# First stage of a decoder layer: context loaded and squared batch by batch, distances sent to DRAM and back per batch

## The reference

```
# 1 linear causal attention with one head of 16, tiled 16 times before the projection
q, k, v = split(x @ qkv_w.T + qkv_b);  wei = where(tril, q @ k.T, 0)
x = layernorm(x + tile(wei @ v, 16) @ proj_w.T + proj_b)
# 2 per batch: Euclidean distances D[77, 256] of context rows to x rows, dynamic time warping over D,
#   backtracking, and the context rows added to the x rows that the path gives them
D = sqrt(max(|c|^2 + |x|^2 - 2 c.x, 0));  R = dtw(D);  path = backtrack(R)
x = layernorm(context_rows_added_along(path) + x)
# 3 product-key memory: batch norm, query, two top-8 of 64, top-8 of 64 pairs, gathered down/up rows
x = layernorm(x + memory(x))
```

## Time and profile before

| | |
|---|---|
| median of 3 runs | 2913.73 us (2905.39 to 2916.35) |
| the profiled execution, its own time | 2907.08 us |
| its span, first to last instruction | 2905.3 us |
| first block | 0 to 201 us of the span |
| first warping row | 207.4 us |
| mean granted TensorE clock | 0.956 of full speed |

### The profile page before, as it was taken

One profiled execution on the slowest core, in us unless ns is written; L12 is line 12 of the kernel. 1 busy time (PEld: TensorE's weight loads), 2 busy tenths in 40 slices (PEclk: granted clock), 3 DMA queues, 4 the chain that ended last, 5 costly groups with the idle time before them and its releaser, 6 DMA issues.

```text
span 2905.3 us, 104629 instructions
## 1 busy us (share of the span) xinstructions
PE 2652.9 (91%) x43108; PEld 2293.1 (79%) x43108; DVE 2210.9 (76%) x7510; ACT 761.9 (26%) x1340; POOL 857.1 (30%) x670
## 2 busy tenths in 40 slices
PE   6961167799999999999999999999999999999996
PEld 5851145688888888888888888888888888888895
DVE  5668966877777777777777777777777778777744
ACT  4740055322222222222222222222222222222210
POOL 1330142233333333333333333333333333333332
PEclk9985589999999999999999999999999999999997
DMA  5550337400000000000000000000000000000000
GB/s 174 172 161 23 65 112 177 72 13 13 11 13 10 13 12 12 13 13 13 14 13 13 13 14 13 13 14 13 13 14 13 13 13 14 13 14 13 10 10 12
DMA packets 84630, 99.34 MB, mean 34 GB/s; under 512 B 6189, under 2 KB 74702, under 8 KB 84046
## 3 DMA queue, kind: packets, MB, share of 16 engines
q1 hardware_dynamic: 84190, 92.94, 11.5%
HBM read 65.13 MB, written 27.79 MB: 32 GB/s over the span
## 4 chain that ended last, share of the span: by engine, by line
PE 82%; issue 7%; DVE 1%; DMA 1%; ACT 1%; POOL 0%; POOLq 0%; DVEq 0%; SPq 0%; ACTq 0%
PE bank L1078 32%; PE bank L1112 31%; PE bank L1096 9%; PE bank L1049 8%; PE bank L767 1%; DMA x_again<-x_scratch 1%; PE bank L770 1%; PE bank L1064 1%; PE bank L1036 1%; DVE hot L1295 0%; ACT x_sb L727 0%; POOL best L664 0%; DMA x_scratch<-x_sb 0%; DVE shared L1307 0%; ACT L1197 0%
## 5 line engine op out<-in xcount | busy, mean ns | idle before, releaser
L1015 POOL TENSOR_TENSOR hot<-hot,valsT 128x512 f32<-128x512 f32 x512 | 733.0, 1451 | 1662.8 <-DVE hot L1295 1662.8
L1078 PE MATMUL bank<-x2T,shared 128*64 128x128 f32 x16384 | 951.4, 274 | 4.6 <-issue 3.1
L1078 PEld LDWEIGHTS bank<-x2T,shared 128*64 128x64 f32 x16384 | 889.8, 137 | 26.6 <-issue 11.9
L1295 DVE TENSOR_TENSOR hot<-places,valsT 128x1024 f32<-128x1024 f32 x512 | 647.6, 1305 | 0.2 <-issue 0.2
L1112 PE MATMUL bank<-up,shared 64*128 64x256 f32 x4096 | 449.4, 379 | 1.5 <-DVE shared L1307 1.5
L1112 PE MATMUL bank<-up,gelh 64*128 64x256 f32 x4096 | 446.4, 377 | 0.0
L1112 PEld LDWEIGHTS bank<-up,shared 64*128 64x128 f32 x4096 | 397.1, 188 | 58.9 <-issue 11.4
L1112 PEld LDWEIGHTS bank<-up,gelh 64*128 64x128 f32 x4096 | 395.2, 187 | 56.2 <-issue 11.5
L1096 PE MATMUL bank<-hot 64*64 64x64 f32 x16384 | 303.1, 224 | 30.9 <-POOL hot L1015 16.3
L1096 PEld LDWEIGHTS bank<-hot 64*64 64x64 f32 x16384 | 267.9, 137 | 79.7 <-issue 79.7
L1307 DVE TENSOR_TENSOR shared<-bank,shared 128x512 f32<-128x512 f32 x256 | 164.7, 685 | 176.8 <-PE bank L1096 176.4
(11 more groups left out here) (151 smaller groups left out, 2169.5 us busy)
## 6 DMA issues: line engine op xcount, KB each, us to landing
x_scratch<-x_sb SPq DMA_DIRECT2D x64, 256.0 KB, 2.1
xT_sb<-in_xT SPq DMA_DIRECT2D x32, 256.0 KB, 2.9
x_sb<-in_x SPq DMA_DIRECT2D x32, 256.0 KB, 3.0
x_again<-x_scratch SPq DMA_DIRECT2D x32, 256.0 KB, 2.8
x_tile<-x_scratch SPq DMA_DIRECT2D x32, 256.0 KB, 3.9
up<-in_table SPq DMA_DIRECT2D x2, 4096.0 KB, 37.0
yo<-x_scratch SPq DMA_DIRECT2D x32, 256.0 KB, 3.0
out_y<-yo SPq DMA_DIRECT2D x32, 256.0 KB, 2.0
```

Source lines behind the costliest of these rows:

```text
L1015: pool.tensor_tensor(lo, lo, valsT[:, par, 2, TQ * q:TQ * (q + 1), None].to_broadcast([P, TQ, NK]), ALU.mult).then_inc(gated_ready, 1)
L1078: mm = pe.matmul(ps_h[q % 2][half(c), i, :], dnT[:, k, lo // 2, half(lo % 2)], x2T[:, par, k, c, :], start=(k == 0), stop=(k == CC - 1))
L1295: dve.tensor_tensor(hot[:, q % SLOTS], places[:, None, None, :].to_broadcast([P, 2, TQ, NK]), valsT[:, par, 0:2, TQ * q:TQ * (q + 1), None ...
```

## The change

It touches the first block and the hand-over to the second.

- Context: instead of four parts, each batch's rows (77 runs of 1 KB) and columns (256 runs of 308 B, into a buffer with two slots) are loaded by two DMAs, `load_ctx`, lag 4 in SyncE's order, last in its step. `norms` squares one batch a step at lag 3; `ctx_scale` at lag 3.
- Distances: after `store_dist` (lag 7) of a batch, `load_cost` (lag 8) waits for that store and loads the batch's distances into their place, `cost[b:P:NB, :]`: four partitions, four runs of 20 KB. The four loads at the start of the second block go; its VectorE waits for no load.
- Lags: TensorE's highest lag is 4 instead of 7, ScalarE's 4 instead of 9, VectorE's 4 instead of 8; orders of the stages in the lists are new; the head's lag is 1 instead of 2. ScalarE's qkv is cut in two (`qk`, `v`) with `std` between. VectorE has four drains in a step instead of two.
- SyncE's code is written out for all steps, with no loop.
- Start: the first xT load comes ahead of the weights; TensorE waits for two early memsets (`pads`) instead of all constants; ScalarE asks for Sqrt once before its data is there; the proj reduction is done in two halves, in VectorE's steps 0 and 1, and attn of batch 0 waits for both.
- `table_init` is raised twice: once after `acc`'s first memsets, which is all the first warping row needs, and once after the rest.

```diff
...
@@ -232,7 +236,7 @@
                 return st.enter_context(nc.sbuf_tensor(name, shape, dt))
             projT = sa("projT", [HS, C * NHEAD])
-            ctx_cols = sa("ctx_cols", [P, CC, NB, S2])
+            ctx_cols = sa("ctx_cols", [P, CC, 2, S2])
             ctxm2 = sa("ctxm2", [P, 2, CC, RP])
             x_sb = sa("x_sb", [P, 2, NT, C])
             xT_sb = sa("xT_sb", [P, 2, CC, T])
@@ -252,7 +256,7 @@
             x1sq = sa("x1sq", [P, CC, T])
             x1sum = sa("x1sum", [P, 2, T])
             dist_sb = sa("dist_sb", [RP, 2, T])
-            sq_scr = sa("sq_scr", [S2, 8, C])
+            sq_scr = sa("sq_scr", [S2, C])
             ps_qkv, ps_v = bank[0][0:2 * GAP + HS, 0:T], bank[6][:, 0:NT * P].rearrange("p (t d) -> p t d", t=NT)
             ps_wei = bank[1][:, 0:3 * P].rearrange("p (k t) -> p k t", k=3)
@@ -272,18 +276,6 @@
                     return ap[bass.ds(b, 1)].rearrange("a p t c -> (a p) t c")
                 def load_xT(b, par):
-                    if isinstance(b, int) and b == 1:
-                        sp.wait_ge(consts, 1)
-                        for dst, src in ((projT[:, :], projT_d), (proj[HS:HS + 1, :], projb_d),
-                                         (gamma[:, :], gamma_d), (beta[:, :], beta_d)):
-                            sp.dma_start(dst, src).then_inc(p_in, 16)
-                    if isinstance(b, int) and 2 <= b < 2 + NB // 8:
-                        some = slice(8 * (b - 2), 8 * (b - 1))
-                        sp.dma_start(ctx_rows[:, some, :], ctx_rows_d[some].rearrange("b s c -> s b c"))\
-                            .then_inc(ctx_in[b - 2], 16)
-                        sp.dma_start(ctx_cols[:, :, some, :],
-                                     ctx_cols_d[:, some].rearrange("(k p) b s -> p k b s", k=CC))\
-                            .then_inc(ctx_in[b - 2], 16)
                     if later(b, 2):
                         sp.wait_ge(qkv_mm, b - 1)
                     sp.dma_start(xT_sb[:, par], one(xTb, b)).then_inc(xT_in[par], 16)
@@ -297,36 +289,59 @@
                     sp.wait_ge(x1_ready, b + 1)
                     sp.dma_start(one(x1b, b), x1_sb[:, par]).then_inc(x1_out[par], 16)
+                def load_ctx(b, par):
+                    if later(b, 2):
+                        sp.wait_ge(norm_seen, b - 1)
+                        sp.wait_ge(ctxm2_ready, b - 1)
+                    sp.dma_start(ctx_rows[:, b, :], ctx_rows_d[b]).then_inc(rows_in[par], 16)
+                    sp.dma_start(ctx_cols[:, :, par, :], ctx_cols_d[:, b].rearrange("(k p) s -> p k s", k=CC))\
+                        .then_inc(cols_in[par], 16)
+
                 def store_dist(b, par):
                     sp.wait_ge(root_ready, b + 1)
-                    sp.dma_start(dist_d[bass.ds(b, 1)].rearrange("a (i j) -> (a i) j", i=RP),
-                                 dist_sb[:, par]).then_inc(dist_out[par], 16)
-
+                    sp.dma_start(dist_d[b].rearrange("(i j) -> i j", i=RP), dist_sb[:, par, :]).then_inc(dist_out[par], 16)
+
+                def load_cost(b, par):
+                    sp.wait_ge(dist_out[par], dmas(b, par))
+                    sp.dma_start(cost[b:P:NB, :], dist_d[b].rearrange("(g f) -> g f", g=NG)).then_inc(cost_in[par], 16)
+
+                load_xT(0, 0)
                 for part in range(3):
                     of = slice(HS * part, HS * (part + 1))
                     at = slice(GAP * part, GAP * part + HS)
                     sp.dma_start(wqkv[:, :, at], wqkvT_d[:, of].rearrange("(k p) d -> p k d", k=CC)).then_inc(w_in, 16)
                     sp.dma_start(bias[at, :], bqkv_d[of]).then_inc(w_in, 16)
-
-                pipeline(sp, [(load_xT, 0), (load_x, 5), (store_x1, 7), (store_dist, 10)], 12)
+                load_xT(1, 1)
+                sp.wait_ge(pads, 1)
+                for dst, src in ((projT[:, :], projT_d), (proj[HS:HS + 1, :], projb_d),
+                                 (gamma[:, :], gamma_d), (beta[:, :], beta_d)):
+                    sp.dma_start(dst, src).then_inc(p_in, 16)
+
+                for i in range(1, NB + 9):
+                    for stage, lag, first in ((load_xT, 0, 2), (load_x, 1, 0), (store_x1, 5, 0), (store_dist, 7, 0),
+                                              (load_cost, 8, 0), (load_ctx, 4, 0)):
+                        if first <= i - lag < NB:
+                            stage(i - lag, (i - lag) % 2)
                 for par in range(2):
                     sp.wait_ge(x1_out[par], 16 * NB // 2)
-                    sp.wait_ge(dist_out[par], 16 * NB // 2)
+                    sp.wait_ge(cost_in[par], 16 * NB // 2)
             @block.gpsimd
             def _(pool):
                 pool.memset(wqkv[:, :, HS:GAP], 0.0)
                 pool.memset(wqkv[:, :, GAP + HS:2 * GAP], 0.0)
+                pool.memset(proj[:, :], 0.0)
+                pool.memset(eps_col[:, :], EPS)
+                pool.drain()
+                pool.nop().then_inc(pads, 1)
                 pool.memset(ones[:, :], 1.0)
                 pool.memset(qT[:, :, :], 0.0)
                 pool.memset(kT[:, :, :], 0.0)
                 pool.memset(vT[:, :, :], 0.0)
                 pool.memset(v_sb[:, :, :, :], 0.0)
-                pool.memset(proj[:, :], 0.0)
                 pool.memset(headT[:, :, :], 1.0)
                 pool.memset(ctxm2[:, :, :, :], 0.0)
                 pool.memset(ctx_norm[:, :], 0.0)
-                pool.memset(eps_col[:, :], EPS)
                 pool.memset(ident[:, :], 0.0)
                 pool.memset(causal[:, :, :], 1.0)
                 pool.iota(iota_i[:, :], [[1, T]], base=0, channel_multiplier=0)
@@ -361,6 +376,8 @@
                 def turn_v(b, par):
                     pe.wait_ge(vT_ready, b + 1)
+                    if not later(b, 1):
+                        pe.wait_ge(consts, 1)
                     if later(b, 1):
                         pe.wait_ge(v_ready, b)
                     for t in range(NT):
@@ -390,7 +407,7 @@
                 def attn(b, par):
                     pe.wait_ge(head_ready, b + 1)
                     if not later(b, 1):
-                        pe.wait_ge(setup_v, 1)
+                        pe.wait_ge(setup_v, 2)
                     if later(b, 1):
                         pe.wait_ge(sum_done, b)
                     for t in range(NT):
@@ -419,19 +436,21 @@
                     pe.wait_ge(sq_ready, b + 1)
                     pe.matmul(ps_dist, ones[:, :], x1sum[:, par, :], start=False, stop=True).then_inc(dist_mm, 1)
-                pe.wait_ge(consts, 1)
+                pe.wait_ge(pads, 1)
                 pe.wait_ge(w_in, 16 * 6)
-                pipeline(pe, [(head, 2), (qkv, 0), (wei, 1), (turn_v, 1), (attn, 3), (turn_x1, 6), (dist, 7)], 10)
+                pipeline(pe, [(qkv, 0), (head, 1), (dist, 4), (wei, 0), (turn_v, 0), (attn, 1), (turn_x1, 2)], 6)
             @block.scalar
             def _(act):
-                def qkv(b, par):
+                def qk(b, par):
                     act.wait_ge(qkv_mm, b + 1)
                     if later(b, 2):
                         act.wait_ge(wei_mm, b - 1)
                     act.activation(qT[0:HS, par, :], ps_qkv[0:HS, :], ACT.Identity, bias=bias[0:HS, :])
                     act.activation(kT[0:HS, par, :], ps_qkv[GAP:GAP + HS, :], ACT.Identity, bias=bias[GAP:GAP + HS, :])\
                         .then_inc(qk_ready, 1)
+
+                def v(b, par):
                     if later(b, 2):
                         act.wait_ge(v_mm, b - 1)
                     act.activation(vT[0:HS, par, :], ps_qkv[2 * GAP:, :], ACT.Identity, bias=bias[2 * GAP:, :])\
@@ -453,14 +472,12 @@
                 def ctx_scale(b, par):
-                    if not later(b, 1):
-                        for part in ctx_in:
-                            act.wait_ge(part, 32)
+                    act.wait_ge(cols_in[par], dmas(b, par))
                     if later(b, 2):
                         act.wait_ge(dist_mm, b - 1)
                     rest(act, act_rests)
                     act.activation(ctxm2[:, par, :, 0:S2],
-                                   ctx_cols[:, :, bass.ds(b, 1), :].rearrange("p k a s -> p k (a s)"),
+                                   ctx_cols[:, :, par, :],
                                    ACT.Copy, scale=-2.0).then_inc(ctxm2_ready, 1)
                 def head(b, par):
@@ -478,9 +495,11 @@
                     act.wait_ge(dist_ready, b + 1)
                     act.activation(dist_sb[:, par, :], dist_sb[:, par, :], ACT.Sqrt).then_inc(root_ready, 1)
+                act.wait_ge(pads, 1)
+                act.activation(sd1[:, 0, 0:1], eps_col[:, :], ACT.Sqrt)
                 act.wait_ge(consts, 1)
                 act.wait_ge(w_in, 16 * 6)
-                pipeline(act, [(root, 9), (head, 2), (qkv, 0), (wei_off, 1), (ctx_scale, 6), (x1_cols, 6), (std, 4)], 12)
+                pipeline(act, [(qk, 0), (std, 2), (v, 0), (head, 1), (wei_off, 0), (ctx_scale, 3), (root, 4), (x1_cols, 2)], 6)
```

(40 more changed lines are left out.)

## The result

The changed kernel takes 2925.86 us in the median (2923.79 to 2927.7, 5 runs) against 2913.15 before: ratio 1.0062, 95% interval 1.0049 to 1.0074. The changed kernel is slower, by some 0.6%, where 2908 us with a range of 2889 to 2920 was forecast. In the profiled executions the span goes from 2905.3 to 2922.8 us, 17.5 more.

A forecast was written before the change was run, and what follows sets the result against it. TensorE bounds the first block at 4.99 us a step; late column loads were to make it 5.57. Earlier hand-over -20.3 plus 14.5 lost gave -5.8 us: 2901.3 profiled, 2908 us by the median, range 2889 to 2920.

The forecast's parts named there:

- What a late column load costs: First block, batches 4 to 28: late context columns delay the residual two steps on; step 5.57 us, 14.5 us lost.
- Rival 4: SyncE's new queue: something else, such as SyncE waiting at the distance load for a store; called cheap; chance 0.05.
- Filling: Start of the first block: first matmul at 5.8 us, first full step (step 4) at 27.9 us.
- Full steps: First block's steps from batch 4: 4.99 us each by the compute engines, 5.57 where the column load is late.
- Emptying and hand-over: End of first block: at 4.99 us a step, VectorE starts the first warping row at 187.1, 20.3 us earlier.
- By the compute engines alone the step stays at 4.99 us; shorter lags cost nothing there: First block's full step: TensorE's work sums to 4.99 us, VectorE's to 4.0, GpSimd's to 1.77.
- The price of 1.53 us: Per-batch distance load: a 20 KB row takes 1.53 us on its DMA engine, ahead of the context columns.
- The gain of 20.3 us: First warping row at 187.1 instead of 207.38 if the first block's step stays at 4.99 us.
- rival 1: The distance load hides: step stays at 4.99 us, 20.3 us gained, 2893 us by the median; chance 0.25.
- rival 2: Context columns' 308-byte runs are dear, 0.1 us each: step 6.25 us, 2925 us by the median; chance 0.12.

The follow-up runs named there:

- e2: Changed kernel without the per-batch distance load, four loads at the start of the second block instead: 2928.48 us, ratio 1.0072 to the kernel before.
- e1: Changed kernel with the distance store one step earlier in SyncE's order (lag 6 instead of 7): 2921.38 us, ratio 1.0046 to the kernel before.
- e9: Changed kernel with four slots and four semaphores instead of two for the distances, SyncE's order untouched: 2923.60 us, ratio 1.0062 to the kernel before.
- e5: Changed kernel with x1 store and distance store ahead of the x load in SyncE's step, lags kept: 2895.53 us, ratio 0.9962 to the kernel before.
- e11: e7 with the scale ahead of `dist` in VectorE's list: 2889.26 us, ratio 0.9945 to the kernel before.
- e7: Changed kernel with both stores ahead of the x load and the context load at lag 3: 2894.74 us, ratio 0.9957 to the kernel before.
- e8: e7 with each batch's distances loaded a second time into unused memory, as four rows of 20 KB: 2917.80 us, ratio 1.0038 to the kernel before.
- e10: e7 with each batch's distances loaded a second time into unused memory, as 80 rows of 1 KB: 2895.16 us, ratio 0.9961 to the kernel before.
- e3: Changed kernel with the distance store at lag 6 and distances loaded at the start of the second block: 2904.40 us, ratio 0.9984 to the kernel before.
- e6: e5 without the per-batch distance load, four loads at the start of the second block instead: 2895.57 us, ratio 0.9962 to the kernel before.

## Why the prediction was wrong

**Which step failed.** The sum that gives the step, under "What a late column load costs": "2p = 5.68 + 5.45 = 11.13 and p = 5.57 us". It is the right working of a ring that comes second. The one on top, VectorE's `dist` waiting for the distance store of b - 2, has a turn of one step, 6.35 us, and was not laid out. In the forecast stores were bytes on the DMA engines and a latency; who waits for their landing was asked for the column load alone. e2 and e1 show it from both sides: the step stays without the distance load, and the wait goes with the store a step earlier; e9 takes the buffer wait away and the step falls to 5.93; e5 shows that the place of the stores behind the waiting x load is the cause.

**Rival 4 was nearest and was priced away.** It put a wait for a store at SyncE and called it cheap, as "stores land in 1.7 us and are issued a step before". Both halves failed. The slot is wanted, for a step of 4.99, 4.99 - 0.68 - 1.72 = 2.59 us after the end of the residual behind which the store is issued; 0.95 of it is gone at the issue, and the store, third in a burst behind x and the x1 store, takes 3.00. With the old 1.7 us the turn would be 0.95 + 1.7 + 1.72 + 0.68 = 5.05 us, by the rows cheap indeed: a landing time was carried over from another order of the queue. And the engine that waits is VectorE, not SyncE.

**Size of each term.** Against the forecast's warping row (187.1 + 14.5 = 201.6) the real one is 26.3 us later:

- Filling: step 4 starts at 28.91, forecast 27.9, +1.0. The first matmul is at 5.42 (5.8).
- Full steps: 200.60 - 28.91 = 171.7 us for 27 steps; forecast 27 x 4.99 + 14.5 = 149.2, +22.5. Nearly the whole miss.
- Emptying and hand-over: 227.90 - 200.60 = 27.3 us; forecast 187.1 - 162.6 (step 31) = 24.5, +2.8. In e11, where no transfer is late, it is 190.11 - 164.08 = 26.0.

The whole missed by less, 2925.86 for 2908: 3.0 us came back in the later blocks, and the forecast had added 6.7 us (0.23%) because the median of three runs of the kernel before lay that far above the profiled one. The medians of that kernel beside the experiments, 2906.15 to 2907.98, don't bear this out, and the changed kernel's median is 1.3 us above its profiled execution (2924.52). So part of the nearness was luck.

**"By the compute engines alone the step stays at 4.99 us; shorter lags cost nothing there"** was wrong too, and covered in the changed kernel by the transfers. e7 has no transfer in its way and a step of 5.24; e11 differs only in VectorE's order and has 4.99. Twenty-seven steps of 0.25 are some 7 us, and the row comes 6.7 us earlier. The busy times were summed (4.0 of 4.99) and ScalarE's order was walked through, but not VectorE's, where the scale stands behind a `dist` that comes late from TensorE. (VectorE's list has three drains in a step, not the four of the description; the sum of 4.0 us loses 0.1 by it.)

**What held.** The long rows of the distance load can be dear for others (e8 against e10), and the column load does arrive late: with the buffer wait away (e9) it sets a step of 5.93, 0.36 above the forecast, from wider spaced issues (+0.41) and a later landing (+0.55), less 0.26 in the series behind, of whose sum a step takes half. The price of 1.53 us that the first distance load put on the columns was too high: without that load they landed 0.9 us sooner in the changed order (e2), 0.5 at store lag 6 (e3 against e1) and 0.1 with the stores first (e6 against e5). It also rests on 40 us for 322 other packets, 0.12 each, where the forecast's own price is 0.05. The gain of 20.3 us without it was close: e11 gets 17.3.

**The rivals.** The distance load (rival 1) cost the step nothing in the changed kernel (6.42 us with it, 6.45 without, e2), because a longer ring stood above it; with the store at lag 6 it cost 0.50 (e1 against e3), and with the stores first nothing, as e5 and e6 are equal. Dear 308-byte runs (rival 2) would have given nearly this time, 2925, for another reason: in e7 and e10 the column load lands in 3.7 and 3.6 us, no later than the 80 KB store before it, and in the changed kernel its wait is the smaller. The Trainium skill (DMA: Bandwidth & Descriptors, "Specifications") wants 512 B for line rate; by those landings nothing of it is seen to reach the time here, and no run changes the run length alone.

**Left open.** The 12.7 us that e9 loses after the first block, and the 3.0 us that the changed kernel regains there.

## What to carry to other kernels

When an issue queue is reordered, write down for every DMA, stores too, who waits for its landing and what in the queue it stands behind; a two-slot buffer turns a late store into a step time. Put an issue whose data is ready ahead of one that waits, and the same on a compute engine's list: one line on SyncE was worth some 29 us, one pair swapped on VectorE brought the first block's end 6.7 us forward. A transfer's landing time before the change is no price for it in another queue, and slack in one ring of a step says nothing of the others.

## What the runs showed of the hardware

- Landing time depended on what stood ahead in the queue: the 80 KB store took 1.7 us before, 2.8 after, 3.8 in e7 and 6.1 in e8.
- 80 KB more a step were free as 80 rows of 1 KB and cost 0.81 us a step as four rows of 20 KB (e10 and e8 against e7), though the mean share of the DMA engines was 80.8% in the first case and 76.5% in the second. The mean share does not show the bottleneck.
- A stage at a DMA share of 79% (e7) ran at 5.24 us a step without a wait for a transfer that counted; one at 63% (after) ran at 6.42, held by a single 80 KB store.
- TensorE's busy time hid lost time. From 110 to 130 us it read 20.00 us in e11 (4.99 us a step, 114 matmul records), 19.80 in e7 (5.24, 108) and 19.66 in e9 (5.93, 100). A busy TensorE is no sign that the stage is at its floor; the distance of two qkv matmuls tells.
